# Routed experts of a one-core transformer layer: output rows in a ring of three, and GpSimd's row scatters released by the rows alone

## The chip, the cores and the metric

One core of one Trainium2 chip. The metric is the device time of one execution in microseconds (us), the median of several executions. The engines are called TensorE (PE in the rows, PEld for its weight loads), VectorE (DVE), ScalarE (ACT), GpSimd (POOL) and SyncE (SP). SyncE issues most of the transfers between HBM and SBUF; GpSimd issues the indirect ones, which write rows to places given by an index.

## The reference, cut to what matters

The input is `x`, 16 sequences of 512 tokens of width 128, so 8192 tokens. An attention layer with relative positions comes first, then a feed-forward layer in which each token goes through one shared expert and through the one of 16 routed experts that its router picks:

```python
x = x + _layernorm(attention(_layernorm(x)))
# the feed-forward layer on h = _layernorm(x):
logits = h @ w_router.T
_, top_idx = jax.lax.top_k(logits, 1)
mask = jax.nn.one_hot(top_idx, 16).sum(axis=1)
scores = sigmoid(logits) * mask
gate_up = einsum('eth,ehf->etf', scores.T[:, :, None] * h[None], gate_up_proj)
gate, up = split(gate_up, 2)
expert_out = einsum('etf,efh->eth', up * silu(gate), down_proj)
shared = silu(h @ w_gate.T) * (h @ w_up.T) @ w_down.T
x = x + _layernorm(shared + expert_out.sum(axis=0))
```

## The kernel before

The program has three stages: the attention, the shared expert (16 units of 512 tokens), and the routed experts, on which the change bears. By then the tokens have been scattered to HBM in the order of their experts (`xs_d`), each expert's rows padded to whole tiles of 128 rows. With 8192 tokens and 16 experts that makes `SORTED` = 80 tiles, whatever the router picks. They are worked off in ten groups of eight (`GROUP` = 8).

For each tile `n` TensorE transposes the rows (L1037), multiplies them with the gate and up weights of their expert (`expert_gates`, L1053) and, two tiles later, with the down weights (`expert_downs`, L1060), which counts the semaphore `y_ps` up by one. ScalarE copies the transposed rows and the expert's weights into place and applies silu (`expert_silu`, L1255). VectorE multiplies gate and up (`expert_hidden`, L1700), adds the shared expert's row (`add_shared`, L1712, counted by `y_ev`) and takes the moments. TensorE's `expert_downs(n)` needs VectorE's `expert_hidden(n)` and `add_shared(n-3)`.

The end of a group also lies on VectorE, spread over its later tiles by `ending`: a reciprocal square root in twelve small steps (`refine`), the destinations of the rows (`places`, L1770 to L1774, into `oidx`), the normalization into the output buffer `og` (`expert_normalize`, L1783, in quarters) and the addition of the residual (`residual`, L1790, in halves). Each half counts `out_rdy` up by one. The list `ENDINGS` cuts the last three groups (7, 8 and 9) into two endings of four tiles each, so that there an ending's half is two tiles. All engines work strictly in the order in which the code issues the instructions.

GpSimd then writes the rows out, one indirect transfer per tile of 128 rows (`store_rows`, L2008): 80 scatters, in order. `og` and `oidx` have two buffers, used by even and odd groups. A buffer of group `g` is written again for group `g+2`, so `places(g+2)` on VectorE waits until all eight scatters of group `g` have landed (`out_st`). A scatter waits for its half (`out_rdy`) and, on top of that, for a count of TensorE's tiles:

```python
pool.wait_ge(m["y_ps"], min(SORTED, GROUP * g + k0 + size + STORE_AT + k))
```

with `STORE_AT` = 12; so row tile 0 goes out after 20 of TensorE's tiles, and those of groups 8 and 9 only after all 80. SyncE loads the rows, the shared expert's rows and the residual rows `x1g` of later groups meanwhile; the load of `x1g` for group `g` (L747) waits until the ending of group `g-2` is done.

## Time and profile before

| | us |
|---|---|
| median of 3 runs | 1648.44 |
| lowest and highest of them | 1647.47, 1655.5 |
| profiled execution, its own time | 1653.81 |
| its span, first to last instruction | 1651.9 |
| stage of the routed experts in it, first silu to end | 1491.5 to 1651.9 |

The rows below come from the profiled execution. Times in them are us from the start of its span. A figure in square brackets at the end of a row is the idle time of the engine ahead of that instruction and what ended it by the profile.

### The profile page before, as it was taken

Reading aid. Unit: us, or ns where it says so; the run is one execution under the profiler, and the core shown is the slowest. Engines: PE = TensorE matmul, PEld = TensorE weight load, DVE = VectorE, ACT = ScalarE, POOL = GpSimd, SP = SyncE. Lnnn points to the kernel's source line nnn. Section 1 sums busy time; section 2 is a strip of 40 time slices with the busy share of each in tenths; the row PEclk is TensorE's granted clock in tenths of the full one; section 3 lists DMA queues with packets and bytes.
Section 4 is the critical chain, followed back from the end, with each engine's and each line's share of the span. In section 5 each row is a group of like instructions: output and inputs, shape, how many; then the busy total and the mean of one; then the engine's idle time right before and its main releaser. Section 6 shows DMA issues by size and latency. Waiting matters only on the chain.

```text
span 1651.9 us, 67945 instructions
## 1 busy us (share of the span) xinstructions
PE 1522.8 (92%) x28642; PEld 1183.3 (72%) x28642; DVE 1226.7 (74%) x3510; ACT 1111.7 (67%) x2053; POOL 485.8 (29%) x678
## 2 busy tenths in 40 slices
PE   5789999999999999999999999999999999899982
PEld 2347777777777777777777777787778676559982
DVE  7996667787878887888787878877885354636885
ACT  4537767776777677767776878687766774328771
POOL 4532030313131313140414041404010112562566
PEclk8999999999999999999999999999999999999996
DMA  3477657765455445445545553545324734225541
GB/s 84 142 194 211 153 152 166 182 165 151 96 146 120 127 110 130 115 127 124 141 91 143 117 146 77 156 108 155 51 72 109 226 82 112 79 98 138 163 143 37
DMA packets 489136, 212.11 MB, mean 128 GB/s; under 512 B 330663, under 2 KB 462436, under 8 KB 488832
## 3 DMA queue, kind: packets, MB, share of 16 engines
q1 hardware_dynamic: 474112, 165.75, 41.1%
q0 software_dynamic: 14720, 42.03, 7.6%
q8 instruction: 225, 3.69, 0.9%
q14 instruction: 79, 0.65, 0.1%
HBM read 105.73 MB, written 102.85 MB: 126 GB/s over the span
## 4 chain that ended last, share of the span: by engine, by line
PE 64%; DVE 15%; issue 6%; SPq 5%; DMA 4%; POOL 3%; ACT 3%; another core or an unknown queue 1%; ACTq 0%; POOLq 0%; DVEq 0%
PE pv L890 11%; PE mix L845 9%; DVE mx L1406 8%; PE sc L868 7%; PE rel L897 7%; PE sc L870 6%; PE mix L847 5%; PE sc L862 4%; PE sc L1053 2%; PE rel L999 2%; PE sc L989 2%; PE pv L990 1%; PE pv L1060 1%; DMA qm_d<-ks 1%; POOL out_dram L2008 1%
## 5 line engine op out<-in xcount | busy, mean ns | idle before, releaser
L1145 ACT ACTIVATE w<-sc,escale 128x512 f32<-128x512 f32 x1024 | 685.0, 689 | 315.7 <-PE sc L870 179.2
L1406 DVE TENSOR_REDUCE mx<-mix 128x1 f32<-128x512 f32 x960 | 643.5, 684 | 198.0 <-PE mix L847 186.1
L845 PE MATMUL mix<-WE 128*32 128x512 f16 (+1 forms) x1968 | 391.6, 395 | 30.4 <-DVE mx L1406 16.5
L890 PE MATMUL pv<-w,shared_part 128*9 128x128 f32 x8192 | 373.1, 273 | 2.8 <-issue 2.8
L847 PE MATMUL mix<-Wn,WE 128*32 128x350 f16 (+41 forms) x1968 | 279.4, 282 | 1.9 <-issue 1.9
L868 PEld LDWEIGHTS sc<-shared_part,Wt 96*128 96x128 f16 x5120 | 220.1, 97 | 84.2 <-issue 33.7
L868 PE MATMUL sc<-shared_part,Wt 96*128 96x64 f16 x5120 | 258.8, 192 | 7.1 <-issue 3.4
L897 PE MATMUL rel<-w,shared_part 128*32 128x128 f32 x5120 | 259.8, 273 | 1.7 <-issue 1.7
L890 PEld LDWEIGHTS pv<-w,shared_part 128*9 128x9 f32 x8192 | 204.8, 90 | 72.4 <-issue 46.8
L870 PE MATMUL sc<-shared_part 104*128 104x128 f16 x2560 | 247.4, 218 | 1.2 <-issue 1.2
L1130 ACT ACTIVATE WE<-qp,hmask 128x256 f16<-128x256 f16 x500 | 215.6, 499 | 22.5 <-PE sc L847 22.5
L845 PEld LDWEIGHTS mix<-WE 128*32 128x32 f16 (+1 forms) x1968 | 144.1, 141 | 83.6 <-DVE mx L1406 59.3
L847 PEld LDWEIGHTS mix<-Wn,WE 128*32 128x32 f16 (+1 forms) x1968 | 153.5, 147 | 18.3 <-issue 4.1
L862 PE MATMUL sc<-shared_part 104*32 104x512 f16 x1536 | 157.3, 385 | 3.2 <-ACT w L1145 1.4
L897 PEld LDWEIGHTS rel<-w,shared_part 128*32 128x32 f32 x5120 | 155.5, 110 | 3.3 <-issue 2.2
L870 PEld LDWEIGHTS sc<-shared_part 104*128 104x128 f16 x2560 | 153.3, 96 | 2.2 <-issue 2.1
L1931 POOL DMA_INDIRECT xs_d<-xs,spot_u x64 | 68.6, 1073 | 255.1 <-PE sc L862 126.8
L2008 POOL DMA_INDIRECT out_dram<-shared_part,oidx x80 | 80.8, 1009 | 68.8 <-PE pv L1060 41.1
L1912 POOL TENSOR_TENSOR rstd<-var,power 128x4 f32<-128x4 f32 x30 | 30.6, 1021 | 223.1 <-DVE var L1300 223.1
L1858 POOL CAST qs<-WE 128x128 f16<-128x128 f32 x60 | 15.2, 295 | 253.4 <-ACT WE L1084 253.4
L1989 POOL DMA_INDIRECT ysh_d<-w,spots x64 | 61.5, 961 | 36.5 <-issue 15.3
L1245 ACT COPY shared_part<-WE 128x768 f32 x80 | 66.7, 838 | 8.1 <-issue 7.8
(263 smaller groups left out, 1940.9 us busy)
## 6 DMA issues: line engine op xcount, KB each, us to landing
qm_d<-ks POOLq DMA_DIRECT2D x48, 512.0 KB, 4.8
shared_part<-qm_d SPq DMA_DIRECT2D x32, 768.0 KB
kt_d<-ks SPq DMA_DIRECT2D x48, 256.0 KB
shared_part<-kt_d SPq DMA_DIRECT2D x128, 96.0 KB
xs_d<-zrow SPq DMA_DIRECT2D x5, 2056.0 KB
vs_d<-vst SPq DMA_DIRECT2D x16, 576.0 KB
shared_part<-vs_d SPq DMA_DIRECT2D x32, 288.0 KB
orl_d<-rel_s SPq DMA_DIRECT2D x512, 8.0 KB
```

What stands on the lines that cost most here:

```text
L845: nc.tensor.matmul(nat[rows, :], lq[:, rows], kn[b2][:, at:at + S], start=True, stop=False, skip_group_check=True)
L847: mm = nc.tensor.matmul(nat[rows, near], le[:, rows], Wn[:, x0:x0 + last - first], start=False, stop=True, skip_group_check=True)
L862: mm = nc.tensor.matmul(bank[keys, :], KC[j][:, b2, q8, 1, keys], qc[:, q8], start=True, stop=True, skip_group_check=True)
L868: nc.tensor.matmul(view[:, :, b, :], Wt[:, x0:x0 + P], qt[:, :, NB * q8 + b, :], start=(b == 0), stop=False, skip_group_check=True)
L870: mm = nc.tensor.matmul(bank[:, P * g:P * g + P], KC[j][:, b2, g, 0, :], qc[:, g, :, 32 * q8:32 * q8 + 32], start=False, stop=(g == 3), sk ...
L890: mm = nc.tensor.matmul(pv[b2][32 * g:32 * g + 9, P * hh:P * hh + P], VC[j][:, b2, 0 if near else 1, h, :], wt[:, :, b2, h, :], start=(j = ...
L897: mm = nc.tensor.matmul(rel[k // 4][32 * q32:32 * q32 + 32, P * (k % 4):P * (k % 4) + P], lv, wt[:, q32, :, :, NU * k:NU * k + NU], start= ...
L1130: ins = nc.scalar.activation(Qb[half][:, :, h, :].rearrange("p e (t b) -> p e t b", t=2), src, ACT.Copy, scale=hmask[:, h:h + 1])
L1145: nc.scalar.activation(weights, products, ACT.Exp, scale=escale[:, 0:1]).then_inc(s["exp_done"], 1)
L1406: nc.vector.tensor_reduce(mx[:, k:k + 1], nat[:], AX.X, ALU.max).then_inc(s["mx_done"], 1)
L1931: pool.indirect_dma_start(xs_d, bass.IndirectOffsetOnAxis(ap=spot_u[:, t:t + 1], axis=0), xs[:, t, :], None).then_inc(scat, 16)
L2008: pool.indirect_dma_start(out.rearrange("b s d -> (b s) d"), bass.IndirectOffsetOnAxis(ap=oidx[g % 2][:, k0 + k:k0 + k + 1], axis=0), og[g ...
```

## The change

The output buffer `og`, its indices `oidx` and the semaphores `out_st` become rings of three (`OUT_RING`). The third `og` lies in a part of the attention's buffer `w1`, which is free in this stage. The wait for `y_ps` is taken out of `store_rows`, with `STORE_AT`. No arithmetic is changed.

```diff
-    og = [part_of_shared(13584 + 1024 * r, GROUP, D) for r in range(2)]
+    og = [part_of_shared(13584 + 1024 * r, GROUP, D) for r in range(2)] + [w_flat[1][:, 0:GROUP * D].rearrange("p (k d) -> p k d", k=GROUP)]
...
-    oidx_f = [sb(f"oidx_f{r}", [P, GROUP]) for r in range(2)]
-    oidx = [sb(f"oidx{r}", [P, GROUP], U32) for r in range(2)]
+    oidx_f = [sb(f"oidx_f{r}", [P, GROUP]) for r in range(OUT_RING)]
+    oidx = [sb(f"oidx{r}", [P, GROUP], U32) for r in range(OUT_RING)]
...
+    out_st = [m[f"out_st{r}"] for r in range(OUT_RING)]
...
         def places(g):
             num = x1g[g % 2][:, :, D]
             dve.wait_ge(x1_ld[g % 2], 16 * (g // 2 + 1))
-            at_least(dve, out_st[g % 2], 16 * GROUP * (g // 2))
+            at_least(dve, out_st[g % OUT_RING], 16 * GROUP * (g // OUT_RING))
...
         def expert_normalize(f, quarter):
                 if k0 == 0:
-                    at_least(dve, out_st[g % 2], 16 * GROUP * (g // 2))
+                    at_least(dve, out_st[g % OUT_RING], 16 * GROUP * (g // OUT_RING))
...
-                ins = nc.vector.tensor_scalar(og[g % 2][:, k, :], yg[g % 2][:, k, :], mv3[g % 2][:, k, 0:1], rstd3[g % 2][:, k:k + 1], ALU.subtract, ALU.mult)
+                ins = nc.vector.tensor_scalar(og[g % OUT_RING][:, k, :], yg[g % 2][:, k, :], mv3[g % 2][:, k, 0:1], rstd3[g % 2][:, k:k + 1], ALU.subtract, ALU.mult)
...
         def store_rows(f):
             for k in range(size):
                 if k % (size // 2) == 0:
                     pool.wait_ge(m["out_rdy"], 2 * f + 2 * k // size + 1)
-                pool.wait_ge(m["y_ps"], min(SORTED, GROUP * g + k0 + size + STORE_AT + k))
-                pool.indirect_dma_start(out.rearrange("b s d -> (b s) d"), bass.IndirectOffsetOnAxis(ap=oidx[g % 2][:, k0 + k:k0 + k + 1], axis=0),
-                                        og[g % 2][:, k0 + k, :], None, bounds_check=TOK - 1, oob_is_err=False).then_inc(out_st[g % 2], 16)
+                pool.indirect_dma_start(out.rearrange("b s d -> (b s) d"), bass.IndirectOffsetOnAxis(ap=oidx[g % OUT_RING][:, k0 + k:k0 + k + 1], axis=0),
+                                        og[g % OUT_RING][:, k0 + k, :], None, bounds_check=TOK - 1, oob_is_err=False).then_inc(out_st[g % OUT_RING], 16)
...
-        for r in range(2):
-            pool.wait_ge(out_st[r], 16 * GROUP * (GROUPS // 2))
+        for r in range(OUT_RING):
+            pool.wait_ge(out_st[r], 16 * GROUP * len(range(r, GROUPS, OUT_RING)))
...
+OUT_RING = 3
...
-STORE_AT = 12
```

On GpSimd, at the end of the program, stand the scatters of group 8 (`oidx0` before, `oidx2` after). Before, the eight of them read:

```order
L2008 DMA out_0_dram<-shared_part,oidx0 8192x128 [waits y_ps,out_rdy,oidx_rdy]
L2008 DMA out_0_dram<-shared_part,oidx0 8192x128 [waits y_ps]
L2008 DMA out_0_dram<-shared_part,oidx0 8192x128 [waits y_ps,out_rdy]
L2008 DMA out_0_dram<-shared_part,oidx0 8192x128 [waits y_ps]
L2008 DMA out_0_dram<-shared_part,oidx0 8192x128 [waits y_ps,out_rdy]
```

And after the change, in the same place:

```order
L2008 DMA out_0_dram<-w1,oidx2 8192x128 [waits out_rdy,oidx_rdy]
L2008 DMA out_0_dram<-w1,oidx2 8192x128
L2008 DMA out_0_dram<-w1,oidx2 8192x128 [waits out_rdy]
L2008 DMA out_0_dram<-w1,oidx2 8192x128
L2008 DMA out_0_dram<-w1,oidx2 8192x128 [waits out_rdy]
```

The wait for `y_ps` is gone from each; number, order and size of the scatters are as they were, and the source of group 8 is now in `w1`.

On VectorE the first instruction of `places` stands once in each group. For groups 2 to 6, as before (L1770; even groups use `x1_ld0`):

```order
L1770 SCALAR_TENSOR_TENSOR oidx_f0<-shared_part,pad 128x8 [waits out_st0,x1_ld0]
L1770 SCALAR_TENSOR_TENSOR oidx_f1<-shared_part,pad 128x8 [waits out_st1,x1_ld1]
L1770 SCALAR_TENSOR_TENSOR oidx_f0<-shared_part,pad 128x8 [waits out_st0,x1_ld0]
L1770 SCALAR_TENSOR_TENSOR oidx_f1<-shared_part,pad 128x8 [waits out_st1,x1_ld1]
L1770 SCALAR_TENSOR_TENSOR oidx_f0<-shared_part,pad 128x8 [waits out_st0,x1_ld0]
```

And after, where the line is L1771:

```order
L1771 SCALAR_TENSOR_TENSOR oidx_f2<-shared_part,pad 128x8 [waits x1_ld0]
L1771 SCALAR_TENSOR_TENSOR oidx_f0<-shared_part,pad 128x8 [waits out_st0,x1_ld1]
L1771 SCALAR_TENSOR_TENSOR oidx_f1<-shared_part,pad 128x8 [waits out_st1,x1_ld0]
L1771 SCALAR_TENSOR_TENSOR oidx_f2<-shared_part,pad 128x8 [waits out_st2,x1_ld1]
L1771 SCALAR_TENSOR_TENSOR oidx_f0<-shared_part,pad 128x8 [waits out_st0,x1_ld0]
```

The instruction stands where it did; it now waits for the scatters of group `g-3` instead of `g-2`.

## Rows read from the trace of the kernel before

**Rows 1.** The page's group of scatters: count, busy us, mean ns, idle before them.

```profile
L2008 POOL DMA_INDIRECT out_dram<-shared_part,oidx x80 | 80.8, 1009 | 68.8 <-PE pv L1060 41.1
```

**Rows 2.** Busy us of the engines by stretch; then clock, DMA share, GB/s.

```profile
core 0: us, PE busy (x) PEld busy (x) DVE busy (x) ACT busy (x) POOL busy (x), PEclk, DMA share, GB/s
...
1630.00:1640.00 10.00, 0.00 (x0) 0.00 (x0) 9.24 (x49) 0.00 (x0) 7.85 (x8) 0.50 0.08 24
1640.00:1652.00 12.00, 0.00 (x0) 0.00 (x0) 0.00 (x0) 0.00 (x0) 7.88 (x8) 0.50 0.03 4
```

**Rows 3.** GpSimd in order of time: start us, us, instruction, idle before.

```profile
1613.69 1.09 POOL L2008 DMA_INDIRECT out_dram<-shared_part,oidx  x1 [1.26 <-PE pv L1060]
...
1622.87 0.98 POOL L2008 DMA_INDIRECT out_dram<-shared_part,oidx  x1 [0.30 <-issue]
1626.00 0.98 POOL L2008 DMA_INDIRECT out_dram<-shared_part,oidx  x1 [2.15 <-remote]
...
1629.90 0.98 POOL L2008 DMA_INDIRECT out_dram<-shared_part,oidx  x1 [0.30 <-issue]
...
1649.32 0.98 POOL L2008 DMA_INDIRECT out_dram<-shared_part,oidx  x1 [0.30 <-issue]
```

**Rows 4.** VectorE in order of time, from group 7's places to the last residual.

```profile
1604.58 0.17 DVE L1770 SCALAR_TENSOR_TENSOR oidx_f<-shared_part,pad 128x8 f32<-128x8 f32 x1 [1.44 <-DMA out_dram<-shared_part,oidx]
...
1605.39 0.41 DVE L1700 TENSOR_TENSOR shared_part<-shared_part,sc 128x256 f32<-128x256 f32 x1
...
1618.76 0.17 DVE L1770 SCALAR_TENSOR_TENSOR oidx_f<-shared_part,pad 128x8 f32<-128x8 f32 x1 [1.92 <-DMA out_dram<-shared_part,oidx]
...
1619.64 0.41 DVE L1700 TENSOR_TENSOR shared_part<-shared_part,rel 128x256 f32<-128x256 f32 x1
...
1620.29 0.46 DVE L1790 TENSOR_TENSOR shared_part<-shared_part 128x256 f32<-128x256 f32 x1
...
1624.90 0.42 DVE L1700 TENSOR_TENSOR shared_part<-shared_part,sc 128x256 f32<-128x256 f32 x1 [3.44 <-issue]
...
1626.78 0.41 DVE L1790 TENSOR_TENSOR shared_part<-shared_part 128x256 f32<-128x256 f32 x1
...
1629.23 0.41 DVE L1790 TENSOR_TENSOR shared_part<-shared_part 128x256 f32<-128x256 f32 x1
...
1639.36 0.42 DVE L1790 TENSOR_TENSOR shared_part<-shared_part 128x256 f32<-128x256 f32 x1
```

**Rows 5.** The chain of work that ended last: start us, us, what.

```profile
1602.30 2.19 DMA out_dram<-shared_part,oidx
...
1611.22 1.68 PE pv L1060 x4
```

**Rows 6.** GpSimd in order of time, scatters of the stage before that wait for nothing.

```profile
1468.05 0.96 POOL L1931 DMA_INDIRECT xs_d<-xs,spot_u  x1 [0.30 <-issue]
1469.31 0.96 POOL L1931 DMA_INDIRECT xs_d<-xs,spot_u  x1 [0.30 <-issue]
```

**Rows 7.** ScalarE in order of time, its silu of tiles 69, 77 and 78.

```profile
1604.20 0.38 ACT L1255 ACTIVATE shared_part<-sc 128x256 f32<-128x256 f32 x1 [2.48 <-remote]
...
1617.99 0.38 ACT L1255 ACTIVATE shared_part<-rel 128x256 f32<-128x256 f32 x1 [2.87 <-PE sc L1053]
1624.48 0.38 ACT L1255 ACTIVATE shared_part<-sc 128x256 f32<-128x256 f32 x1 [6.11 <-remote]
```

**Rows 8.** Waits from 1495 to 1655: us in total, times, longest us.

```profile
ACT shared_part L1255 <- PE sc L1053: 12.6, 9, 2.9
ACT shared_part L1255 <- remote: 8.6, 2, 6.1
ACT shared_part L1255 <- PE rel L1053: 3.5, 3, 1.9
```

**Rows 9.** Busy us in one microsecond, columns as in Rows 2.

```profile
1623.00:1624.00 1.00, 0.00 (x0) 0.00 (x0) 0.00 (x0) 0.00 (x0) 0.85 (x1) 0.50 1.09 325
```

**Rows 10.** VectorE's residual addition of 512 columns, in order of time.

```profile
1537.25 0.68 DVE L1790 TENSOR_TENSOR shared_part<-shared_part 128x512 f32<-128x512 f32 x1
```

**Rows 11.** GpSimd at the same moment, in order of time.

```profile
1537.31 1.50 POOL L2008 DMA_INDIRECT out_dram<-shared_part,oidx  x1 [1.58 <-PE pv L1060]
```

More of the change, by code:

```diff
@@ L307, in attention_phase @@
     m = a["moe_sem"]
-    xs_ld, x1_ld, ysh_ld, out_st = ([m[f"{n}{r}"] for r in range(2)] for n in ("xs_ld", "x1_ld", "ysh_ld", "out_st"))
+    xs_ld, x1_ld, ysh_ld = ([m[f"{n}{r}"] for r in range(2)] for n in ("xs_ld", "x1_ld", "ysh_ld"))
+    out_st = [m[f"out_st{r}"] for r in range(OUT_RING)]
     names = ("w_ld w_ld2 w_ld3 tab act_zero bnd_ps rk_ps qb_dve wn_ld pool_set dve_set act_set pe_set sp_set wt_ld rv_ld zeroed kc_zeroed "
@@ L1768, in places @@
             dve.wait_ge(x1_ld[g % 2], 16 * (g // 2 + 1))
-            at_least(dve, out_st[g % 2], 16 * GROUP * (g // 2))
-            nc.vector.scalar_tensor_tensor(out=oidx_f[g % 2][:], in0=num, scalar=0.0, in1=pad[:], op0=ALU.is_equal, op1=ALU.mult).then_inc(m["oidx_step"], 1)
+            at_least(dve, out_st[g % OUT_RING], 16 * GROUP * (g // OUT_RING))
+            nc.vector.scalar_tensor_tensor(out=oidx_f[g % OUT_RING][:], in0=num, scalar=0.0, in1=pad[:], op0=ALU.is_equal, op1=ALU.mult).then_inc(m["oidx_step"], 1)
             dve.wait_ge(m["oidx_step"], 2 * g + 1)
-            nc.vector.scalar_tensor_tensor(out=oidx_f[g % 2][:], in0=num, scalar=1.0, in1=oidx_f[g % 2][:], op0=ALU.subtract, op1=ALU.max).then_inc(m["oidx_step"], 1)
+            nc.vector.scalar_tensor_tensor(out=oidx_f[g % OUT_RING][:], in0=num, scalar=1.0, in1=oidx_f[g % OUT_RING][:], op0=ALU.subtract, op1=ALU.max).then_inc(m["oidx_step"], 1)
             dve.wait_ge(m["oidx_step"], 2 * g + 2)
-            nc.vector.tensor_copy(oidx[g % 2][:], oidx_f[g % 2][:]).then_inc(m["oidx_rdy"], 1)
+            nc.vector.tensor_copy(oidx[g % OUT_RING][:], oidx_f[g % OUT_RING][:]).then_inc(m["oidx_rdy"], 1)
         def expert_normalize(f, quarter):
@@ L1789, in residual @@
             tiles = slice(k0 + size // 2 * half, k0 + size // 2 * (half + 1))
-            nc.vector.tensor_tensor(og[g % 2][:, tiles, :], og[g % 2][:, tiles, :], x1g[g % 2][:, tiles, 0:D], ALU.add).then_inc(m["out_rdy"], 1)
+            nc.vector.tensor_tensor(og[g % OUT_RING][:, tiles, :], og[g % OUT_RING][:, tiles, :], x1g[g % 2][:, tiles, 0:D], ALU.add).then_inc(m["out_rdy"], 1)
         def ending(f, step, third):
@@ L2059 @@
 MOE_SEMS = ("scat we_ld cnt_ps2 cnt_step eid_rdy iotas xs_ld0 xs_ld1 x1_ld0 x1_ld1 ysh_ld0 ysh_ld1 sT_ps sT_ev we_done gu_ps silu_done "
-            "h_done y_ps y_ev sum0 st0_step mv0_step st_step mv_step dve_passed2 pool_passed2 fin_step root3 oidx_step oidx_rdy out_rdy out_st0 out_st1")
+            "h_done y_ps y_ev sum0 st0_step mv0_step st_step mv_step dve_passed2 pool_passed2 fin_step root3 oidx_step oidx_rdy out_rdy out_st0 out_st1 out_st2")
+OUT_RING = 3
 RING = 7
```

## The prediction

> **What bounds the kernel now.** The change touches only the stage of the routed experts, so that stage alone was read. The page's group of scatters comes first: 80 of them, 80.8 us busy, 1009 ns each [rows 1]. That is the work of one engine over a stage of 160 us, so GpSimd is not the bound of the stage as a whole. Who is the bound at its end is in the stretches: from 1630 to 1640 TensorE does nothing, VectorE is busy for 9.24 us and GpSimd for 7.85; from 1640 on VectorE has nothing either and GpSimd alone works [rows 2]. So the kernel ends with a queue of scatters, which the order of time shows one by one: the scatter at 1629.90 is the first of group 8, the last of all starts at 1649.32, and 15 steps lie between them, 1.295 us each [rows 3]. The last rows had been ready since 1639.36 + 0.42 = 1639.8 [rows 4]. Group 8's first scatter is thus what to ask about: its two tiles were ready at 1626.78 + 0.41 = 1627.2, but scatters of group 7 still ran until 1629.6 [rows 3, 4].
>
> Further up the stage is carried by VectorE and TensorE. Twice in it VectorE stops at L1770, `places`, until scatters have landed: 1.44 us at 1604.58 (group 7) and 1.92 us at 1618.76 (group 8) [rows 4]. The chain names what it hangs on the first time: a scatter issued at 1602.30 took 2.19 us to land [rows 5].
>
> **The change, part by part.** The sum is made against the profiled execution's own time, 1653.81 us (span 1651.9), which is 5.4 above the median of the runs, 1648.44; the differences are then taken off the median.
>
> *Instructions.* 80 waits leave GpSimd's program, one `places`-wait and nothing else leaves VectorE's; no work is added. What a wait per scatter costs is seen where there is none: the last scatters of `xs_d` start 1.26 us apart with nothing to wait for, 0.30 of it idle [rows 6], and the scatters that the change touches leave the same 0.30 between them when their waits are long fulfilled [rows 3]. I take nothing for it; 16 scatters at the shorter period would end 16 x 0.035 = 0.6 us sooner, which is the upper bound.
>
> *The wait for TensorE's count, end of the program.* Without it group 8's scatters need only their rows, and those of group 7 go out earlier. Group 7's last two tiles were ready at 1620.29 + 0.46 = 1620.75 [rows 4]. The scatters ahead of them, the last of which started at 1622.87 [rows 3], are let go some two tiles earlier in the new kernel, and the last two start at 1620.75 + 0.8 = 1621.5 and are over by 1621.5 + 2 x 1.295 = 1624.1. So at 1627.2 GpSimd stands idle and takes group 8's first rows at once. At once is not zero: the scatter at 1613.69 started 0.8 us after TensorE's chain step that released it had ended (1611.22 + 1.68 = 1612.90) [rows 3, 5]. Group 8 then begins at 1627.2 + 0.8 = 1628.0 in place of 1629.90, a gain of 1.9 us. Behind it the queue is as dense as before, since VectorE finishes faster than GpSimd issues: the tightest pair is the second, added at 1629.23 + 0.41 = 1629.64, plus 0.8 is 1630.4, and its turn comes at 1628.0 + 2 x 1.295 = 1630.6; the eighth is ready at 1639.8 for a turn at 1646.1. With 16 scatters of 1.295 each after it the end moves by the same **1.9 us** (2.7 if the start followed without delay, 0 if GpSimd had another stop like the unexplained 2.15 us ahead of 1626.00 [rows 3] at this place).
>
> *The wait for TensorE's count, body of the stage.* There the scatters run some two tiles behind their rows, which costs nothing: what hides it is that the next group's rows come only every eight tiles. Eight scatters take 8 x 1.295 = 10.4 us. If that cover went, they would be late as at the end.
>
> *The ring of three.* `places` of group 7 then waits for group 4 and that of group 8 for group 5, both landed long before. The 1.44 us at 1604.58 don't come back whole: ScalarE's silu of tile 69 ended at 1604.20 + 0.38 = 1604.58, and `expert_hidden` of that tile, behind `places` on VectorE, started at 1605.39 [rows 4, 7]. It could start at about 1604.6: **0.8 us**. The 1.92 at 1618.76 likewise: `expert_hidden` of tile 77 started at 1619.64, and its silu ended at 1617.99 + 0.38 = 1618.37, so it comes 1.2 us earlier with silu where it is, 2.0 with silu 0.8 earlier [rows 4, 7]. What is late next is ScalarE itself: silu of tile 78 starts only at 1624.48, after 6.11 us of idleness that no engine ends, and VectorE stands for 3.44 us until it [rows 4, 7]. The profile names no engine of this core as what it waited for. If this stop keeps its place in time, the whole gain of the ring is lost here (0); if it keeps its length, 0.8 gets through; if it depends on the load of `x1g` that `residual` at 1620.29 releases and that moves 325 GB/s at 1623 [rows 9], it moves with VectorE, by 1.2 to 2.0. I take **0.8**, between them.
>
> Such stops of ScalarE run through the stage: its silu waits 14 times, 12.6 + 8.6 + 3.5 = 24.7 us in all, 1.8 us each, mostly under the names of engines that had finished [rows 8]. The change doesn't remove their cause as far as the trace tells, so they are what can scatter the result.
>
> *New place of the third buffer.* Same partitions, same size, same instructions: nothing, hidden or not. It would cost only if VectorE or the transfers had to wait for `w1`'s last readers, and those belong to the stage before.
>
> *GpSimd beside VectorE.* A half's scatters now start just behind its residual addition, beside VectorE's next normalizations. The rows show what this can cost: a scatter that started 0.06 us after a residual addition of 512 columns took 1.50 us in place of 0.98 [rows 10, 11], while the mean over all 80 is 1009 ns [rows 1], so there are few. The first scatter of a half now starts after that addition instead of in it, which would spare such an overlap; in the tail none was long. I take 0. The Trainium skill (SBUF — State Buffer, "Who interferes with whom") says that VectorE in its two-port modes, such as a `tensor_scalar`, and GpSimd lock each other out of a shared port for the whole instruction. The slow scatter agrees that something of the kind exists here; by the rule read strictly the normalizations too would hold up the scatters that now run beside them.
>
> **Sum.** 1.9 + 0.8 = 2.7 us: the profiled execution would take 1651.1, and the median 1648.44 - 2.7 = **1645.7 us**. The likeliest case's own range is from 1.9 + 0 to 2.7 + 2.0 gained, 1643.7 to 1646.5.
>
> **The rivals.**
> *The stops shrink* (chance 0.2). If silu of tile 78 stopped 1.8 us like the mean of the others and not 6.11, or several of the stops depended on how scatters and loads meet, 4.3 us more come off: 1641.4. For it speaks that the highest of the runs of before is 8 above the lowest with the same program, so an execution can lack such a stop; against it, that the median presumably lacks the long one already. It passes 0.5% (8.2 us) if three more of the small ones go too: 2.7 + 3 x 1.8 = 8.1.
> *Nothing comes through* (0.1). The stop at 1624.48 stays in place and GpSimd's own stop of 2.15 us moves to the front of group 8: 1648.4.
> *The bursts hurt* (0.15), the case on the other side. The scatters of a half, let go as soon as their rows are there, fall into the loads of the next groups, and each meeting adds a stop of 1.8 us on ScalarE, behind which VectorE and TensorE wait. With three more stops it is 1648.44 - 2.7 + 5.4 = 1651.1; slower than before from the second on (2.7 / 1.8 = 1.5), slower by 0.5% from the seventh (10.9 / 1.8 = 6.1). For it speaks that ScalarE's two longest stops lie at the end, one of them ending with a load at 325 GB/s [rows 7, 9]; against it, that number and size of the transfers stay and eight scatters fill 10.4 us of a group in either kernel.
> *The shared port.* If each of the 16 last scatters ran 0.52 us longer beside VectorE, as the one of 1.50 did [rows 11], the end would come 8.3 - 2.7 = 5.6 us later than before: 1654.0. Chance 0.03, since VectorE works beside eight of those 16 already [rows 2], none of them long. This is the page's rule at its strictest.
>
> **How the numbers follow.** The likeliest case has 0.52. The range reaches to the first rival's 1641.4 and a little beyond, 1640, and to the third's three stops, 1651. About 0.5% is what a measurement of this kernel can tell from no change. Faster by more needs the first rival and three stops: 0.09. Slower by more needs seven stops, or the port and more: 0.05. The rest, 0.86, is within it.
>
> **What the profile of the changed kernel would show.** Right: L1771 without a wait for a transfer; GpSimd idle ahead of group 8's first scatter, released by a residual addition; 15 steps of 1.29 to 1.30 us behind it; the last scatter 21 to 22 us after the ready rows of group 8. Scatters of group 0 start by VectorE's release, not TensorE's. Wrong: if the last scatter starts less than 20 us after them, the period hung on the waits; if ScalarE's silu waits add up to far from 24.7 us, the stops depend on the scatters, and the forecast fails by their difference.

## The result, and the profile after

The change made the kernel slower: 1688.22 us (1685.26 to 1694.74, six runs) against 1652.55 us (1647.47 to 1657.02, six runs), a ratio of 1.0217 [1.0192, 1.0242]. Forecast were 1645.7 us and a range up to 1651. The profiled execution after took 1687.56 us, with a span of 1685.8 at a mean granted clock of 0.966 (before: 1653.81, 1651.9 and 0.979).

The stage of the routed experts, counted from its first silu to the end of the span, grew from 160.4 us to 195.7. Its first silu starts at 1490.1 us after and 1491.5 before, so the loss lies wholly in this stage.

A single scatter costs what it did. The page has 56 of the 80 in one group, which answers to [rows 1] (989 ns each, 1009 before):

```profile
L2008 POOL DMA_INDIRECT out_dram<-shared_part,oidx x56 | 55.4, 989 | 78.6 <-DVE shared_part L1791 62.4
```

Both parts of the edit did what the code says. VectorE's `places` (L1771) never waits any more; in the view of its line nothing stands under its idle time:

```profile
L1771 DVE SCALAR_TENSOR_TENSOR oidx_f<-shared_part,pad x10: 155/160/161, 1515.3 to 1668.6; 128x8 f32<-128x8 f32 x10
its engine sat idle before it (us, times) until:
```

And the scatters now start by VectorE's residual addition and run eight in a row. This is GpSimd's timeline after; the last column is its idle time ahead of each scatter, and `...` stands for rows left out:

```profile
1521.12 1.00 POOL L2008 DMA_INDIRECT out_dram<-shared_part,oidx  x1 [22.23 <-DVE shared_part L1791]
...
1538.85 0.98 POOL L2008 DMA_INDIRECT out_dram<-shared_part,oidx  x1 [7.70 <-DVE shared_part L1791]
1540.14 0.98 POOL L2008 DMA_INDIRECT out_dram<-shared_part,oidx  x1 [0.30 <-issue]
...
1547.86 0.98 POOL L2008 DMA_INDIRECT out_dram<-shared_part,oidx  x1 [0.31 <-issue]
...
1560.03 0.98 POOL L2008 DMA_INDIRECT out_dram<-w,oidx  x1 [11.19 <-DVE w L1791]
...
1663.42 0.98 POOL L2008 DMA_INDIRECT out_dram<-w,oidx  x1 [0.65 <-issue]
...
1683.05 0.98 POOL L2008 DMA_INDIRECT out_dram<-shared_part,oidx  x1 [0.30 <-issue]
```

Eight scatters from 1538.85 to 1548.8 with nothing but 0.30 us between them, then 11.19 us of rest. Before, the same work was broken up by the removed wait, from 1532 to 1613 into runs of mostly three or four scatters with gaps of mostly 1.3 to 1.8 us. A piece of GpSimd's timeline before shows it:

```profile
1537.31 1.50 POOL L2008 DMA_INDIRECT out_dram<-shared_part,oidx  x1 [1.58 <-PE pv L1060]
1539.12 0.98 POOL L2008 DMA_INDIRECT out_dram<-shared_part,oidx  x1 [0.30 <-issue]
1540.41 0.98 POOL L2008 DMA_INDIRECT out_dram<-shared_part,oidx  x1 [0.30 <-issue]
1541.70 0.98 POOL L2008 DMA_INDIRECT out_dram<-shared_part,oidx  x1 [0.30 <-issue]
1544.19 0.98 POOL L2008 DMA_INDIRECT out_dram<-shared_part,oidx  x1 [1.51 <-PE pv L1060]
```

What else happens during a run of eight is in ScalarE's timeline after, over the same stretch:

```profile
1540.95 0.26 ACT L1251 COPY shared_part<-mix 128x128 f32<-128x128 f32 x1
1542.47 0.38 ACT L1256 ACTIVATE shared_part<-sc 128x256 f32<-128x256 f32 x1 [1.26 <-PE sc L1054]
1543.11 0.83 ACT L1246 COPY shared_part<-WE 128x768 f32 x1 [0.25 <-issue]
1547.52 0.27 ACT L1251 COPY shared_part<-mix 128x128 f32<-128x128 f32 x1 [3.58 <-remote]
1550.37 0.38 ACT L1256 ACTIVATE shared_part<-sc 128x256 f32<-128x256 f32 x1 [2.59 <-PE sc L1054]
```

ScalarE stands still for 3.58 us ahead of a copy that takes 0.27, and the profile names no engine of this core for it; right behind comes a second long stop, ahead of a silu. The first and short one, 1.26 us ahead of the silu at 1542.47, began at 1541.21, which is 2.4 us into the run. In the stage's seven long runs the first stop begins 1.9 to 2.7 us behind the run's first scatter.

TensorE's rows show the work that the two long stops wait for, the transposed rows and the gates of those tiles:

```profile
1541.28 0.27 PE L1038 MATMUL mix<-ident,shared_part 128*128 128x128 f32 x1
1541.39 1.06 PE L1054 MATMUL sc<-w,shared_part 128*128 128x128 f32 x8
```

The transpose is over at 1541.55 and the gates at 1542.45. The trace also records when a semaphore is raised. The count that the copy waits for is raised at 1547.50, and the copy starts at 1547.52; the count for the silu is raised at 1550.35, and the silu starts at 1550.37. So ScalarE is ready, and what is late is the count of TensorE's work, by 5.9 and 7.9 us.

The windows of the same place show who pays, busy time of each engine in 4 and in 8 us:

```profile
core 0: us, PE busy (x) PEld busy (x) DVE busy (x) ACT busy (x) POOL busy (x), PEclk, DMA share, GB/s
1538.00:1542.00 4.00, 4.00 (x38) 4.00 (x38) 3.78 (x19) 2.67 (x7) 2.54 (x3) 1.00 0.84 228
1542.00:1550.00 8.00, 4.58 (x30) 4.11 (x29) 1.11 (x7) 1.48 (x3) 5.32 (x6) 0.82 0.43 125
```

Before 1542 TensorE is full and VectorE nearly so. Behind it VectorE works for 1.11 us of 8 and TensorE for 4.58, and TensorE's granted clock falls to 0.82 after its pauses. The core's transfers move less in that stretch, not more (228 and 125 GB/s). The view of waits over 1495 to 1690 says the same as a sum (us in all, times, the longest); its silu lines answer to [rows 8]:

```profile
DVE shared_part L1701 <- ACT shared_part L1256: 47.4, 23, 6.8
ACT shared_part L1256 <- remote: 16.8, 4, 4.7
ACT shared_part L1256 <- PE sc L1054: 14.4, 12, 2.7
ACT shared_part L1256 <- PE rel L1054: 11.5, 8, 3.1
ACT shared_part L1251 <- remote: 9.5, 4, 3.6
```

Silu's waits were 24.7 us [rows 8] and are 16.8 + 14.4 + 11.5 = 42.7. VectorE waits 47.4 us for silu now and waited 17.1 before:

```profile
DVE shared_part L1700 <- ACT shared_part L1255: 17.1, 18, 2.2
```

For what follows I call a *stop* the time by which a silu or a copy of rows starts later than everything that it needs: the end of the silu or copy before it on ScalarE, of the tile's matmuls (by TensorE's rows, not by their count), and of `expert_hidden` two tiles earlier. Counted over the stage, above 0.3 us each, silu's stops and the copies' stops came to 24.2 and 4.3 us before, and to 36.8 and 14.4 after. That is 22.7 us more, of 35 lost. The rest was not traced to single rows; what lies behind a stop in other engines, and matmuls at a lower clock, are what could make it.

How late counts are can be read for all of them. TensorE raises three in this stage, for transposes, gates and `expert_downs`. I call a raise *late* if it comes more than 0.15 us behind the latest matmul of its kind that had ended. That is how late it is at the least; behind its own matmul it can be more, like the 7.9 us above. Before, 107 of 218 recorded raises are late, by up to 7.1 us, and after 86 of 223, by up to 6.7 us. No raise by a silu, a copy or an `expert_hidden` comes more than 0.01 us behind in either. (A matmul's end is modelled in the trace, and some raises are missing from it.) Of the 26 stops after, 24 end 0.02 us behind the raise of the very count of TensorE's that was awaited, and 17 of the 19 before.

### The profile page after: what moved, and what is told of

Read it like the earlier page. It is cut to its first block, busy times and chain, and to the rows that moved or that the text cites. A ratio compares the mean times of both kernels' runs of the same rounds, so it can differ in the third digit from the quotient of the medians.

```text
span 1685.8 us, 67928 instructions
## 1 busy us (share of the span) xinstructions
PE 1537.7 (91%) x28642; PEld 1199.8 (71%) x28642; DVE 1227.7 (73%) x3510; ACT 1113.2 (66%) x2053; POOL 484.9 (29%) x678
## 4 chain that ended last, share of the span: by engine, by line
PE 65%; DVE 17%; issue 6%; DMA 3%; POOL 3%; ACT 2%; SPq 2%; another core or an unknown queue 2%; ACTq 0%; POOLq 0%; DVEq 0%
PE pv L891 12%; PE mix L846 10%; DVE mx L1407 9%; PE sc L869 8%; PE rel L898 7%; PE sc L871 6%; PE mix L848 5%; PE sc L863 4%; PE sc L1054 2%; PE rel L1000 1%; PE sc L990 1%; ACT w L1146 1%; PE pv L991 1%; DMA qm_d<-ks 1%
## 5 line engine op out<-in xcount | busy, mean ns | idle before, releaser
L1131 ACT ACTIVATE WE<-qp,hmask 128x256 f16<-128x256 f16 x500 | 215.6, 499 | 20.2 <-PE sc L848 20.2
L2008 POOL DMA_INDIRECT out_dram<-shared_part,oidx x56 | 55.4, 989 | 78.6 <-DVE shared_part L1791 62.4
```

What stands on the lines that cost most here:

```text
L1131: ins = nc.scalar.activation(Qb[half][:, :, h, :].rearrange("p e (t b) -> p e t b", t=2), src, ACT.Copy, scale=hmask[:, h:h + 1])
```

## The experiments

Each group was run on one chip beside the kernel before. They turned out to be chips of two kinds, which matters for all readings: on chips A and C, and where the result above was measured, the kernel before takes 1649 to 1653 us, and the traces show stops; on chips B, D and E it takes 1614 to 1616 us, and none of the traces kept there (none is of the kernel before) shows a stop of silu. Each chip was used for one group only, so a lasting difference of the chips and one of the occasion aren't told apart.

### Chip A: which part of the change, and does ScalarE's own load matter?

The kernel before took 1649.38 us here (13 runs). **e1_ring_wait_kept**, the ring of three with the removed wait put back:

```diff
+                pool.wait_ge(m["y_ps"], min(SORTED, GROUP * g + k0 + size + STORE_AT + k))
+STORE_AT = 12
```

> The ring of three with the third buffer in w1, and the wait for TensorE's count put back. Theory A (a run of scatters without gaps holds up ScalarE, and the wait for the count had put gaps into it): as before, ratio 1.00 (0.995 to 1.005), ScalarE's silu stops near 25 us in the stage. Theory B (the third buffer in w1 or the longer ring is what costs): near the changed kernel, 1.02.

**e2_wait_removed_only**, the kernel before without that wait, buffers two deep as they were:

```diff
-                pool.wait_ge(m["y_ps"], min(SORTED, GROUP * g + k0 + size + STORE_AT + k))
```

> The kernel before with the wait for TensorE's count taken out, two buffers as before. Theory A: about the changed kernel, ratio 1.02 (+36 us), seven stops of ScalarE of 5 to 8 us. Theory B: as before, 1.00.

**e3_fixed_expert_ids**, the changed kernel in which ScalarE reads no expert number into a register ahead of each weight copy (tiles use wrong experts, sizes stay):

```diff
-            e = act.value_load(eid[0:1, n:n + 1], min_val=0, max_val=E - 1)
-            nc.scalar.copy(we[n % RING], WE[:, bass.ds(e, 1), :].rearrange("p o n -> p (o n)")).then_inc(m["we_done"], 1)
+            nc.scalar.copy(we[n % RING], WE[:, n // 5:n // 5 + 1, :].rearrange("p o n -> p (o n)")).then_inc(m["we_done"], 1)
```

> The changed kernel in which ScalarE copies the weights of expert n/5 for tile n, so without reading the expert's number from SBUF into a register (computation changed: tiles use the wrong experts, all sizes the same). Theory C (it is ScalarE's register load that the scatters hold up, as only ScalarE has one in this stage): the stops vanish, ratio 0.99 or below. Theory D (ScalarE is held up whatever it does, by its instructions or semaphores being late): stops as in the changed kernel, ratio 1.015 to 1.02.

**e4_plain_stores_by_sync**, the changed kernel with the rows written by plain transfers of one tile on SyncE's queue (they land in the experts' order, padding rows too):

```diff
+                sp.dma_start(out.rearrange("b s d -> (b s) d")[P * n:P * n + P, :], og[g % OUT_RING][:, k0 + k, :]).then_inc(out_st[g % OUT_RING], 16)
...
-        for f in range(len(ENDINGS)):
-            store_rows(f)
```

> The changed kernel with the 80 indirect scatters of GpSimd replaced by 80 plain stores of the same size on SyncE's queue (computation changed: rows go out in the experts' order). Theory E (the written rows' traffic holds up ScalarE): stops remain. Theory F (GpSimd's making of the descriptors, or its queue, does it): ScalarE's stops of more than 3 us vanish and the stage ends 30 to 45 us sooner than in the changed kernel.

| | us (runs from, to) | ratio to before | stage, us | stops, silu and copies, us |
|---|---|---|---|---|
| e1 | 1650.03 (1643.32, 1654.15) | 0.9998 [0.998, 1.0016] | 158.8 | 23.9, 3.9 |
| e2 | 1683.61 (1681.69, 1686.16) | 1.0207 [1.0185, 1.023] | 196.0 | 34.8, 14.7 |
| e3 | 1678.16 (1671.1, 1681.88) | 1.0182 [1.0157, 1.0206] | 187.5 | 37.1, 16.2 |
| e4 | 1621.95 (one) | not timed in rounds | 132.4 | 0.5, 0.4 |

The removed wait alone brings a loss as large as the whole change did (e2), and the ring alone is worth nothing that can be measured (e1). ScalarE's register load isn't what stops it (e3); the waits of silu in e3 still read:

```profile
ACT shared_part L1255 <- PE sc L1054: 22.1, 26, 3.4
ACT shared_part L1255 <- remote: 18.3, 7, 4.0
ACT shared_part L1255 <- PE rel L1054: 7.7, 12, 2.4
```

e4 says that the stops belong to the scatters, and not only those that the change added: e1, with the wait, has 23.9 + 3.9 us of stops on this chip, e4 0.5 + 0.4. Without scatters the stage takes 132.4 us, 28 less than before, with no fewer bytes written. Of the 28, 19 lie ahead of the last `expert_downs` (117.5 us after the first silu, before 136.3); the other 9 are GpSimd's queue at the end, which is gone too. Its lines of the same view:

```profile
DVE shared_part L1718 <- ACT shared_part L1273: 8.3, 15, 1.1
ACT shared_part L1273 <- PE sc L1071: 3.5, 7, 1.0
```

That leaves open whether it is the written rows or GpSimd's making and issuing of them.

### Chip B: the rows or the issuing, and softer waits

**e5_rows_dropped** gives the scatters indices out of bounds, so that each is made and issued but writes nothing:

```diff
-            nc.vector.tensor_copy(oidx[g % OUT_RING][:], oidx_f[g % OUT_RING][:]).then_inc(m["oidx_rdy"], 1)
+            nc.vector.tensor_copy(oidx[g % OUT_RING][:], pad[:]).then_inc(m["oidx_rdy"], 1)
```

> The changed kernel with every destination out of bounds, so that the scatters are issued and their descriptors made, but no row is written (the output rows are left out). Theory F1 (ScalarE is held up while GpSimd makes descriptors without gaps): stops near the 37 us of the changed kernel, time about 1685. Theory F2 (the small writes and their completion do it, through the DMA engines): stops under 10 us, time about 1640.

**e6_plain_stores_by_gpsimd** lets GpSimd issue a plain transfer for each tile instead (rows in the experts' order):

```diff
+                pool.dma_start(out.rearrange("b s d -> (b s) d")[P * n:P * n + P, :], og[g % OUT_RING][:, k0 + k, :]).then_inc(out_st[g % OUT_RING], 16)
```

> The changed kernel with GpSimd's 80 indirect scatters replaced by 80 plain stores of the same size on GpSimd's own queue (computation changed: rows go out in the experts' order). Theory F1 in its wide form (any transfer whose descriptors GpSimd makes): stops as in the changed kernel, if they too take about 1 us each back to back. Narrow form (only the indirect instruction): few stops, time 1622 to 1640.

**e7_count_two_tiles_earlier** is e1 with the count eased:

```diff
+                pool.wait_ge(m["y_ps"], min(SORTED, GROUP * g + k0 + size + STORE_AT + k))
+STORE_AT = 10
```

> Ring of three and the wait for TensorE's count kept, but with 10 for 12, so each scatter goes two tiles earlier, still one per tile. Theory A (it is the gaps that count, not how late the scatters go): 0.995 to 1.005 of before, stops 20 to 30 us. Theory G (it is the time at which they go, into the loads and VectorE's endings): between, 1.01.

**e8_count_once_per_four** is e1 with the wait ahead of every fourth scatter only:

```diff
+                if k % 4 == 0:
+                    pool.wait_ge(m["y_ps"], min(SORTED, GROUP * g + k0 + size + STORE_AT + k))
```

> Ring of three, the wait for TensorE's count (12) only ahead of every fourth scatter, so that they go in fours without a gap between. Theory A with a threshold near 4 us of unbroken scatters: nearly as before, 1.00 to 1.007, since before they go in threes and fours too. Theory H (each wait taken out costs, by the share of waits taken out): 1.015.

Before took 1615.16 us here (19 runs), 34 less than on chip A. e5 took 1605.94 and e6 1598.48 (one run each); e7 took 1610.35 (1604.36 to 1613.8), ratio 0.9964 [0.9946, 0.9981]; e8 took 1612.19 (1604.38 to 1620.6), ratio 0.9982 [0.9955, 1.0008]. In all four no silu ever stops (0.0 us; 0.4 for copies), and no count of TensorE's in the stage comes more than 0.01 us behind its matmul. So e5 and e6 tell nothing of the cause here, and missed their purpose: with e7 and e8 free of stops too, there was nothing for them to take away. The same kernels had to be tried elsewhere. Nor can e7 and e8 say what an earlier or rarer wait does where there are stops.

### Chip C: the same questions where there are stops

**f1_changed_again** is the changed kernel unaltered, **f2_rows_dropped** and **f3_plain_stores_by_gpsimd** are e5 and e6.

> The changed kernel itself, beside the kernel before on one chip. The chip of the first four experiments ran the kernel before in 1649 us, that of the next four in 1615, with no stop of ScalarE in either of their profiled kernels. Theory I (the stops, and with them the loss, are a matter of the chip): on a chip of 1615 the ratio is 0.995 to 1.0, my first sum of -2.7 us; on one of 1649 it is 1.02. Theory J (the loss is there on every chip): 1.02 on either.

> The changed kernel with all rows of the scatters out of bounds, so issued but not written (output left out), again, beside the changed kernel on its chip. On a chip with stops: F1 (making descriptors holds ScalarE up) stops of 30 us or more and a time like the changed kernel's; F2 (the writes do) stops under 10 us and 30 us less. On a chip without stops: no difference over 5 us.

> The changed kernel with plain stores on GpSimd's queue for the indirect ones (rows in the experts' order), again, beside the changed kernel on its chip. On a chip with stops: if descriptors of any kind made on GpSimd do it, stops remain; if only the indirect form, none. On a chip without stops 5 to 10 us less than the changed kernel, since a plain store holds GpSimd for less.

**f4_pause_per_two** is the changed kernel with a rest of GpSimd after every second scatter, a small clear and a wait for it:

```diff
+                if k % 2 == 1:
+                    paused[0] += 1
+                    pool.memset(zrow[:, 0:64], 0.0).then_inc(m["pause"], 1)
+                    pool.wait_ge(m["pause"], paused[0])
```

> The changed kernel in which GpSimd, after every second scatter, clears 64 unused columns and waits for that, without asking for TensorE's count. On a chip with stops: theory A (gaps on GpSimd, whatever makes them, let ScalarE go on) stops near the 24 us of the kernel before, time 10 to 35 us under the changed kernel; theory K (it is the tie to TensorE's tiles that helps, not the gap) stops as in the changed kernel. On a chip without stops: 0 to 15 us more than the changed kernel, by the pauses in the last 16 scatters.

| | us | stage, us | stops, us |
|---|---|---|---|
| before (7 runs) | 1652.61 | | |
| f1 | 1687.87 (1683.25, 1690.32), ratio 1.0202 [1.0157, 1.0246] | 197.5 | 34.7, 18.9 |
| f2 | 1683.24 (one) | 196.1 | 35.8, 16.5 |
| f3 | 1624.73 (one) | 133.4 | 0.7, 1.2 |
| f4 | 1652.46 (one) | 164.0 | 5.8, 4.6 |

f2 writes no row and stops as f1 does. Its run of eight on GpSimd, and ScalarE in the middle of it:

```profile
1533.52 0.98 POOL L2008 DMA_INDIRECT out_dram<-shared_part,oidx  x1 [7.00 <-DVE shared_part L1791]
...
1542.55 0.98 POOL L2008 DMA_INDIRECT out_dram<-shared_part,oidx  x1 [0.30 <-issue]
```

```profile
1538.61 0.38 ACT L1256 ACTIVATE shared_part<-sc 128x256 f32<-128x256 f32 x1 [2.63 <-PE sc L1054]
1542.21 0.27 ACT L1251 COPY shared_part<-mix 128x128 f32<-128x128 f32 x1 [2.14 <-remote]
```

So neither the rows' writes to HBM nor their meeting with loads do it: GpSimd's queue moved 0.05 MB for these scatters and not 4.2. What is left of a scatter without rows is GpSimd's work on it and as many packets as before, 2560, with next to nothing in them. In f3 GpSimd issues as many transfers, of as many packets with data, in 543 ns each and not 989, and next to nothing stops. Whether it is the indirect kind as such or that each holds GpSimd for longer isn't told apart. From f3's page, and the largest lines on silu in its waits:

```profile
L2009 POOL DMA_DIRECT2D out_dram<-shared_part x56 | 30.1, 543 | 59.7 <-DVE shared_part L1791 58.0 <-issue 1.6
```

```profile
DVE shared_part L1701 <- ACT shared_part L1256: 7.8, 14, 1.1
ACT shared_part L1256 <- PE sc L1054: 2.4, 4, 1.0
```

The counts tell the same. f2 has 88 of 222 late, up to 6.7 us. f3 still has the indirect scatters of the stage before: from 1380 to 1489 us 37 of TensorE's 92 recorded raises are late, and from 1500 on, after the last of those scatters (1497), none of 215 is.

f4 is the test of the run's length: the same 80 scatters, rows and releases, only never more than two without a rest of 0.8 us. Its stops fall from f1's 34.7 + 18.9 to 5.8 + 4.6 us. TensorE's counts are late as often as ever, 99 of 213, but by 1.9 us at most. GpSimd's timeline and the waits in f4:

```profile
1541.38 0.98 POOL L2010 DMA_INDIRECT out_dram<-shared_part,oidx  x1 [0.79 <-issue]
1542.66 1.12 POOL L2010 DMA_INDIRECT out_dram<-shared_part,oidx  x1 [0.30 <-issue]
1543.76 0.19 POOL L2014 MEMSET zrow<- 128x64 f32 x1
1544.75 0.98 POOL L2010 DMA_INDIRECT out_dram<-w,oidx  x1 [0.79 <-issue]
```

```profile
DVE shared_part L1701 <- ACT shared_part L1256: 17.5, 16, 6.1
ACT shared_part L1256 <- PE sc L1054: 5.8, 9, 1.5
ACT shared_part L1251 <- remote: 1.5, 1, 1.5
```

Its last `expert_downs` starts 120.5 us after the first silu (before 136.3, after 172.7). But the end gains nothing from that: two scatters and a rest take 3.24 us, 1.62 a scatter and not 1.29, so GpSimd has a backlog when TensorE is through at 1607.2 and works on it until 1650.6. The stops were turned into a queue of GpSimd's.

### Chip D: a rest only where it isn't in the way of the end

**g1_pause_per_two_body** keeps f4's rests for the first 48 tiles, **g2_pause_per_four_body** has one after four scatters:

```diff
+                if GROUP * g + k0 + k < 48 and (k0 + k) % 2 == 1:
+                    pause()
```

```diff
+                if GROUP * g + k0 + k < 48 and (k0 + k) % 4 == 3:
+                    pause()
```

> The changed kernel with GpSimd's pause (clear 64 unused columns, wait for it) after every second scatter, for the first 48 tiles only, so that the scatters behind the last tiles go without pauses. Theory A with a gap of about 1 us per two scatters: stops of ScalarE about 10 us in the stage on a chip with stops, GpSimd 24 pauses x 0.65 = 16 us later at most in the body and none at the end: 1636 to 1643 where before is at 1650, ratio 0.990 to 0.996. Rival K: 1.00 or above. On a chip without stops 0.99 to 1.00.

> As the last, with the pause after every fourth scatter. If a run of 5.2 us without a gap already holds ScalarE up (the stops of the changed kernel began some 4 us into a run): stops between those of the kernel before and of the pause per two, 15 to 25 us, ratio 0.995 to 1.00. If a single gap frees ScalarE altogether: as the pause per two or better.

**g3_pause_also_in_shared_stage** is g1 with a rest after every second of the shared expert's scatters too (`scatter_unit`), **g4_clear_without_wait** is g1 with a clear of eight columns and no wait behind it:

```diff
+                if t % 2 == 1:
+                    pause()
```

```diff
+            pool.memset(zrow[:, 8 * (paused[0] % 32):8 * (paused[0] % 32) + 8], 0.0).then_inc(m["pause"], 1)
```

> As the pause per two, and the 64 scatters of the shared expert's rows in the stage before are paused in the same way. If that stage loses time by the same cause (on the chip of 1615 us the routed stage started 34 us sooner than on that of 1649): 10 to 30 us less than with the pause in the last stage alone, ratio 0.975 to 0.99. If not: 0 to 5 us more, as the pauses delay the loads behind those scatters.

> As the pause per two in the body, but GpSimd clears 8 columns and does not wait for it, so no idle gap of 0.8 us follows. If any other instruction between scatters frees ScalarE: stops about 10 us, 1640 where before is at 1650. If the idle gap is needed: stops of 30 us or more, 1680.

Before took 1614.36 us here (22 runs), and no silu stopped in any of the four traces, so this too was a chip without stops. g1: 1621.53 (1618.6 to 1633.6), ratio 1.0054 [1.0027, 1.008]. g2: 1612.13 (1607.61 to 1619.94), 0.9984 [0.9961, 1.0007]. g3: 1621.56 (1616.54 to 1629.74), 1.0049 [1.0029, 1.0069]. g4: 1609.65, one run. Where there is nothing to cure, 24 rests cost 0.5%; 12 cost nothing that can be told. g4, which asked whether any instruction between two scatters is enough, stays without an answer.

### Chip E: what the change is worth without stops

**h1_changed_third_time** is the changed kernel unaltered, **h2_pause_per_four_body** is g2.

> The changed kernel once more, unaltered, since it has not yet met a chip without the stops. Theory I (the loss is a matter of the chip): where the kernel before takes about 1615 us, ratio 0.994 to 1.000 and no stop of ScalarE over 1 us; where it takes about 1650, 1.02 again. Theory J: 1.02 on either.

> The changed kernel with GpSimd's pause after every fourth scatter of the first 48 tiles, again, on the chip of the changed kernel. On a chip with stops: between the kernel before and the changed one, 0.995 to 1.01, with stops of 15 to 30 us (runs of 5.2 us against 10.4); on one without, 0.998 as measured.

Once more a chip without stops (before 1615.85 us, 19 runs), which served for the one thing not yet known there. h1: 1610.6 (1605.12 to 1613.33), ratio 0.9977 [0.9953, 1.0002], which is 3.7 us by that ratio (the two medians lie 5.3 apart). h2: 1611.14 (1607.21 to 1617.13), ratio 0.9971 [0.9949, 0.9992]. The very same program is 2% slower than before on one kind of chip and as fast or a little faster on the other. In h1 GpSimd's runs are even longer. These are the last fourteen of a run of sixteen scatters, and ScalarE works in the middle of it as if there were none:

```profile
1494.70 0.98 POOL L2008 DMA_INDIRECT out_dram<-shared_part,oidx  x1 [0.30 <-issue]
...
1511.65 0.98 POOL L2008 DMA_INDIRECT out_dram<-shared_part,oidx  x1 [0.30 <-issue]
```

```profile
1506.95 0.39 ACT L1256 ACTIVATE shared_part<-rel 128x256 f32<-128x256 f32 x1
1507.50 0.83 ACT L1246 COPY shared_part<-WE 128x768 f32 x1 [0.16 <-issue]
1508.24 0.26 ACT L1251 COPY w<-mix 128x128 f32<-128x128 f32 x1
```

```profile
core 0: us, PE busy (x) PEld busy (x) DVE busy (x) ACT busy (x) POOL busy (x), PEclk, DMA share, GB/s
1500.00:1510.00 10.00, 10.00 (x92) 10.00 (x91) 9.86 (x54) 8.84 (x22) 7.87 (x8) 1.00 0.76 212
```

TensorE full, VectorE 9.86 of 10 and ScalarE 8.84 beside eight scatters. The window of 1542 to 1550 above is its counterpart. None of TensorE's 237 recorded raises in h1's stage is more than 0.01 us behind.

## Why the prediction was wrong

**The step that failed** is the one on "the wait for TensorE's count, body of the stage": there the scatters "run some two tiles behind their rows, which costs nothing". As a wait it does cost nothing, and e1 shows that keeping it loses nothing. But it did something that I didn't ask about: it cut GpSimd's work into runs of three or four scatters. Taken away, it left runs of eight, 10.0 us long, and beside them TensorE's counts came up to 6.7 us late and more, so that ScalarE stopped, with VectorE and TensorE behind it. The term that stood at nothing cost 35 us. Shown by: e2 (the wait alone brings 1.0207), e4 and f3 (no indirect scatters, hardly a stop), f2 (no rows written, stops as in f1), f4 (a rest per two scatters, a fifth of the stops). Of these e4, f2, f3 and f4 are one run each, with effects of 28 us and more or, in f2, none.

**ScalarE's stops.** I took their 24.7 us for background: "the change doesn't remove their cause as far as the trace tells". They came with the very instruction that the change lets go. I had the row with the largest, 6.11 us with no engine of this core named [rows 7], and GpSimd's runs beside it [rows 3], and didn't lay all stops against all scatters: right ahead of that largest stop, from 1613.69 to 1623.85, stands the one run of eight that the body of the stage has before. That would have asked the right question: what else shortens or lengthens such a run? I also took the names that the profile gives, mostly TensorE's matmuls, for those of engines "that had finished". The matmuls had finished; their counts had not come. For the largest stop the gates of tile 78 ended at 1616.91, and their count was raised at 1624.46, just ahead of the silu at 1624.48. The text said what would prove it wrong, silu's waits "far from 24.7 us"; they came out at 42.7.

**The rival on the right side** was "the bursts hurt", chance 0.15. It had the sign, the victim and the followers right, and the mechanism and the size wrong. The mechanism was given as scatters that meet loads, so that number and size of transfers, which stay, spoke against it; f2 has it that the rows don't matter. The size was one stop of 1.8 us at each of three meetings, the mean of the stops behind short runs; behind runs of eight there were 22.7 us more of them in all, and 35 us by the length of the stage. The argument that eight scatters fill 10.4 us of a group in either kernel was true and beside the point: they filled it in pieces.

**The ring of three** was sized right as a mechanism and lost in the result. Both waits at L1771 are gone, but the 0.8 us that I let through can't be seen: e1 stands at 0.9998 [0.998, 1.0016]. It isn't at fault for anything either.

**The tail** came as forecast on this chip, and not on chip E. Group 8's first half was ready at 1662.16 + 0.41 = 1662.57 by this row of `residual`:

```profile
1662.16 0.41 DVE L1791 TENSOR_TENSOR w<-w,shared_part 128x256 f32<-128x256 f32 x1
```

Its first scatter started at 1663.42, 0.85 later (forecast 0.8). GpSimd had stood idle ahead of it, though for 0.65 us only and not for 3.9, and the profile names "issue" and not the residual addition. Then 15 steps of 19.63 / 15 = 1.309 us follow to 1683.05 (forecast 1.29 to 1.30; three of the scatters are long ones, of 1.04 to 1.13 us). From the ready rows to that last start it is 20.5 us, where before had 22.1, so 1.6 of the 1.9 us are there. (The forecast's own terms, 0.8 + 15 x 1.295, give 20.2 to the last start; its "21 to 22" fits the end of that scatter, 21.5.) But group 7's rows came late here, behind stops, and so left GpSimd free. In h1, without stops, they didn't:

```profile
1578.31 0.41 DVE L1791 TENSOR_TENSOR w<-w,shared_part 128x256 f32<-128x256 f32 x1
1581.44 0.98 POOL L2008 DMA_INDIRECT out_dram<-w,oidx  x1 [0.30 <-DVE w L1791]
```

The last 32 scatters are one run there, and group 8's first waits 2.7 us for its turn, as it did before. The forecast had let group 7's last scatters start with their rows and had not counted GpSimd's queue from group 6 on. So this term is worth nothing on chip E. The 3.7 us of the whole change there, whose interval reaches past zero, lie near the 2.7 of the sum by luck: what makes them, if they are there, no run shows.

**The shared port** played no part: the scatters of the tail took 0.98 to 1.13 us beside VectorE's normalizations, and none is 0.52 longer.

**What stays open.** Why some chips stop and others don't, and whether it is the chip or the occasion. Why TensorE's counts come late, and only TensorE's: the matmuls' ends are modelled, so the traces don't tell whether the matmuls themselves end late or only the news of them. Whether a rest is needed or any instruction would do (g4 met a chip without stops). How long a run may be: runs of two leave 10.4 us of stops (f4), runs of mostly three and four 28.5 (before), runs of eight 51.2 (after), but a rest per four (g2, h2) never met a chip with stops.

The stage before is open in part. On the chips with stops the first silu comes at 1482 to 1492 us, on the others at 1457 to 1466, and the shared expert's scatters are as dense. TensorE's counts are late there too: from 1380 us to the first silu 45 of 98 recorded raises before, up to 8.2 us, and none of 98 in h1. How much of the 30 us that makes wasn't measured.

No version with the right output beat both kernels on chips with stops: e1 ties with before, and so does f4 with its one run. On chips without, e7 has the lowest ratio, 0.9964 [0.9946, 0.9981], which h1's and h2's intervals overlap, and it wasn't run on the other kind.

## What to carry to other kernels

A wait that nobody is kept waiting by costs nothing, and still it may pace what its engine sends; before taking it out, look at the run lengths it makes (here 3 or 4 scatters with gaps of 1.3 to 1.8 us) and at what other engines do during the longest run. Idle time that the profile puts down to no engine, or to one that had long finished, is not background: look when the awaited count was raised, and lay such places against the instructions of each other engine before calling them independent of the change. And compare within one chip: 34 us lay between two chips for the same program, and a change had two signs on them.

## What the runs showed of the hardware

On some chips counts that TensorE raises come late while GpSimd issues indirect scatters back to back (0.98 us busy, 0.30 between): 86 of 223 in the stage after, by 6.7 us and more, and ScalarE, which waits for them, stands still for 2 to 5 us at a time. The counts that ScalarE and VectorE raise came within 0.01 us in the same traces. The first stop begins 1.9 to 2.7 us into such a run, and with runs of two the counts are 1.9 us late at most (f4). It needs neither written rows (f2) nor the third buffer (e2). Behind the last indirect scatter it ends: plain transfers issued by GpSimd, 543 ns each, left none of 215 counts late (f3). In the first 300 us of the kernel before, without an indirect transfer, none of 574 of TensorE's counts is late. On other chips sixteen such scatters in a row leave ScalarE at 8.84 us of 10 and no count late (h1). The Trainium skill (SBUF — State Buffer, "Who interferes with whom") says that TensorE and ScalarE never wait on anyone among the engines' ports. The traces agree so far as they tell: what ScalarE waits for in after's long stops is a semaphore count that isn't there yet, and in h1 its silus don't stop at all (0.0 us).

Beside it the granted clock of TensorE went from 1.00, which is 2.4 GHz, in the stretch from 1538 to 1542, in which it was busy throughout, to a mean of 0.82 in the next 8 us, in which it had idled for 3.4; a part of these 8 us thus ran at 1.2 GHz. How much of the loss that makes was not measured.
